# Gated attention with a routed layer behind it: the negated score maxima of a batch kept in one padded 128-column tile and turned by one product instead of four

## What is computed

```
Q = (layernorm(x) @ Wq.T + bq)            # 16 heads of 32
K, V = (ctx @ Wk.T + bk), (ctx @ Wv.T + bv)
attn = softmax(Q K^T / sqrt(32))
x = x + tanh(g_xattn) * ((mean_e(attn V @ We.T + be)) @ Wo.T + bo)
...
best = argmax(softmax(layernorm(x) @ w_gate)); place = running count of best
x = x + tanh(g_ffn) * gate * (layernorm(x) @ w_expert + b_expert)   # where place < 100
```

## Time and profile before

| | us |
|---|---|
| median of 3 runs | 409.02 |
| lowest and highest run | 408.29, 409.28 |
| span of the profiled execution | 406.7 |

### The profile page before, as it was taken

One profiled execution on the slowest core, in us unless ns is written; L12 is line 12 of the kernel. 1 busy time (PEld: TensorE's weight loads), 2 busy tenths in 40 slices (PEclk: granted clock), 3 DMA queues, 4 the chain that ended last, 5 costly groups with the idle time before them and its releaser, 6 DMA issues.

```text
span 406.7 us, 8772 instructions
## 1 busy us (share of the span) xinstructions
PE 400.1 (98%) x3126; PEld 190.6 (47%) x3126; DVE 336.5 (83%) x683; ACT 228.2 (56%) x320; POOL 167.0 (41%) x154
## 2 busy tenths in 40 slices
PE   8999999999999999999999999999999999999996
PEld 4556664444444444444444444444444444454444
DVE  6549566986897989988998999899897688779996
ACT  4435423678556764946585485748556473876110
POOL 2027999224171157309034530803261063460371
PEclk9999999999999999999999999999999999999999
DMA  7999991464058408814860683286059016241585
GB/s 266 319 388 396 366 382 39 104 126 148 2 129 194 158 12 168 233 68 98 145 236 2 149 228 106 65 175 240 0 131 238 9 33 172 79 135 27 96 167 185
DMA packets 65517, 63.19 MB, mean 155 GB/s; under 512 B 41765, under 2 KB 45233, under 8 KB 65475
## 3 DMA queue, kind: packets, MB, share of 16 engines
q1 hardware_dynamic: 60363, 56.19, 50.7%
q0 software_dynamic: 1632, 3.49, 3.2%
q10 hardware_dynamic: 3480, 2.96, 2.2%
HBM read 29.59 MB, written 12.98 MB: 105 GB/s over the span
## 4 chain that ended last, share of the span: by engine, by line
PE 93%; DVE 2%; ACT 1%; DMA 1%; issue 1%; SPq 0%; POOL 0%; ACTq 0%; DVEq 0%
PE ps L840 76%; PE ps L456 9%; PE ps L588 3%; PE ps L405 2%; DMA ctx_raw<-in_ctx_dram 1%; ACT probs L1237 1%; ACT mixT_hi L397 0%; SPq L729 0%; PE ps L1164 0%; DVE xb L1570 0%; DVE wqT_lo L1680 0%; DVE mixT_lo L398 0%; POOL known L1931 0%; PE ps L606 0%; PE ps L525 0%
## 5 line engine op out<-in xcount | busy, mean ns | idle before, releaser
L1237 ACT ACTIVATE probs<-ps 120x1024 f32<-120x1024 f32 x64 | 62.0, 1024 | 21.8 <-PE ps L840 21.7
L1604 DVE TENSOR_REDUCE neg_max<-ps 128x16 bf16<-128x1920 f32 x32 | 68.6, 2143 | 3.7 <-PE ps L840 3.7
L1990 POOL TENSOR_TENSOR attn_lo<-attn,attn_hi 128x512 f16<-128x512 f32 x28 | 31.8, 1158 | 91.3 <-ACT attn_hi L1237 91.3
L840 PE MATMUL ps<-xnT_hi,wqT_hi 128*128 128x512 f16 x128 | 48.6, 380 | 0.0
L840 PE MATMUL ps<-mixT_hi,attn_hi 128*128 128x512 f16 x128 | 48.6, 380 | 0.0
L840 PE MATMUL ps<-mixT_lo,attn_hi 128*128 128x512 f16 x128 | 48.5, 379 | 0.0
L840 PE MATMUL ps<-xnT_lo,wqT_hi 128*128 128x512 f16 x128 | 48.5, 379 | 0.0
L1998 POOL TENSOR_TENSOR xb<-xb,mix_bias 128x512 f32<-128x512 f32 x32 | 39.6, 1270 | 15.1 <-DVE cb_col L1547 15.1
L1237 ACT ACTIVATE q_hi<-ps,bias_cols 128x512 f16<-128x512 f32 x32 | 22.1, 689 | 31.5 <-PE ps L840 31.5
L840 PE MATMUL ps<-q_stack,k_stack 97*120 97x512 f16 x128 | 35.0, 390 | 1.2 <-DMA q_stack<-shift 0.7
L840 PE MATMUL ps<-probs,den_sel 120*32 120x256 f32 x512 | 34.1, 384 | 0.0
(11 more groups left out here) (277 smaller groups left out, 807.0 us busy)
## 6 DMA issues: line engine op xcount, KB each, us to landing
xb<-in_x_dram SPq DMA_DIRECT2D x8, 1024.0 KB, 7.0
q_stack<-q_hi SPq DMA_DIRECT2D x48, 128.0 KB, 2.4
out_dram<-xb SPq DMA_DIRECT2D x6, 1024.0 KB, 6.7
raw<-in_L_xattn_We_dram SPq DMA_DIRECT2D x5, 1024.0 KB, 11.2
q_stack<-q_lo SPq DMA_DIRECT2D x32, 128.0 KB, 2.6
xb<-in_L_xattn_We_dram SPq DMA_DIRECT2D x3, 1024.0 KB, 10.1
k_stack<-k_scratch SPq DMA_DIRECT2D x8, 360.0 KB, 4.4
k_scratch<-k_hi ACTq DMA_DIRECT2D x16, 120.0 KB, 7.2
```

Of the source, the lines that this page charges most:

```text
L840: return e.matmul(out_, a, b, start=start, stop=stop, **kw)
L1237: return e.activation(out_, in_, func, **kw)
L1604: e.tensor_reduce(neg_max[:, :, :, g], quad[:, :, 0:NT * SK].rearrange("p j (t s) -> p t j s", t=NT), AX.X, ALU.max, negate=True).then_inc ...
L1990: e.tensor_tensor(attn_lo[:, g, :], attn[:, g, :], attn_hi[:, g, :], ALU.subtract).then_inc(s_alo, 1)
```

## The change

- `neg_max` becomes one tile of 128 x 128 bf16. Columns 0 to 63 hold the maxima in the order (j, g, t), columns 64 to 127 are zeroed once at the start by GpSimd (one more MEMSET; the count SET that others wait for goes from 16 to 17).
- The reduction writes the same 16 numbers with other distances.
- max_turn is one product with all 128 columns as weights; its output is 128 x 128, of which 64 partitions matter.
- shift_row reads 64 x 128 instead of 16 x 512.
- The transfer into row 96 of `q_stack` reads 64 partitions of 256 bytes instead of 16 of 1024.

```diff
-        neg_max = sb("neg_max", [P, NT, HJ, NK], BF16)
-        shift = sb("shift", [H, S], F16)
+        neg_max = sb("neg_max", [P, P], BF16)
+        shift = sb("shift", [NT * H, P], F16)
...
-        SET, SETV, N_CONST = 16, 21, 1
+        SET, SETV, N_CONST = 17, 21, 1
...
-                    load(q_stack[3 * DK:STACK, :, :, :].rearrange("o j g s -> o (j g) s"),
+                    load(q_stack[3 * DK:STACK, :, :, :].rearrange("o j g (t s) -> o (j g t) s", s=P),
                          shift[:, :], s_rsh)
...
-                for t in range(NT):
-                    ins = mm(den_b[0:H, t * P:(t + 1) * P], neg_max[:, t, :, :].rearrange("p j g -> p (j g)"),
-                             ident_bf[:, :])
-                ins.then_inc(s_mt, 1)
+                mm(den_b[:, 0:P], neg_max[:, :], ident_bf[:, :]).then_inc(s_mt, 1)
...
-                act(shift[:, :], den_b[0:H, :], scale=1.0 / SHIFT_UNIT).then_inc(s_sh, 1)
+                act(shift[:, :], den_b[0:NT * H, 0:P], scale=1.0 / SHIFT_UNIT).then_inc(s_sh, 1)
...
-                e.tensor_reduce(neg_max[:, :, :, g], quad[:, :, 0:NT * SK].rearrange("p j (t s) -> p t j s", t=NT),
+                maxed = neg_max[:, 0:NT * H].rearrange("p (j g t) -> p t j g", j=HJ, g=NK)
+                e.tensor_reduce(maxed[:, :, :, g], quad[:, :, 0:NT * SK].rearrange("p j (t s) -> p t j s", t=NT),
                                 AX.X, ALU.max, negate=True).then_inc(s_mx, 1)
...
+            made_const(e.memset(neg_max[:, NT * H:P], 0.0))
```

## The result

The changed kernel takes **407.13 us** (median of 21 runs, 406.5 to 408.3); the kernel before, run beside it, takes 408.33 (407.8 to 409.38). The ratio is 0.9972 with a 95% interval from 0.9966 to 0.9978: 1.14 us less, certain in sign, and just under the 0.3% that a single comparison can tell. Forecast were 0.80 us less. The forecast time of 408.2 started from the 409.02 of three runs; from 408.33, the median of 21, the same 0.80 gives 407.5. The profiled execution after has a span of 405.5 us (before 406.7). The ratios of this document leave out three runs that fell far above the rest (415.65 and 588.33 of the kernel before, beside e1 to e4, and 1034.96 of e6).

A forecast was written before the change was run, and what follows sets the result against it. The prediction took TensorE (PE), busy for 98% of the span, as the bound, with DVE second in batches 2 to 6. It summed 0.30 + 5 x 0.12 - 0.10 = 0.80 us, so 409.02 - 0.8 = 408.2, range 406.9 to 409.2.

The forecast's parts named there:

- The turn, 0.30: PE at max_turn: one full-array product, without the 128*128 to 128*16 border, lets the next product start 0.30 us earlier.
- Batch 0, nothing kept: The product behind the turn waits for a part of sum_lo from DVE, not for the turn: 0 gained.
- Batch 1, 0.30: Scores of group 1 wait for exponentials that follow scores(1, 0), so everything behind moves along: 0.30 us kept.
- Batches 3 to 6, 0.12 each: At table_rows PE waits for DVE's place_hot, leaving 0.04; scores of group 1 return 0.08 to 0.10: 0.12 us each.
- Batch 2, 0.12: Same DVE limit at table_rows, with the shift's issue moving from 158.44 to about 157.91: 0.12 us kept.
- Batch 7, nothing kept and -0.10: scores(7, 0) waits for the shift's transfer, so the turn gives 0 and the slower transfer costs 0.10 us.
- Transfer +0.1: Shift into q_stack: 64 rows of 256 bytes take 0.1 us longer, hidden in batches 1 to 6, lost in batch 7.
- wide load 0: PE at the turn: loading 128 columns of weights instead of 16 costs nothing.
- The base, 409.02: Median time of the kernel before that the saving was subtracted from; the measured time was put 2.3 us above the span.
- A: Rival: DVE isn't second, six batches keep 0.30 to 0.36; 406.6 to 407.2 us; chance 0.20.
- B: Rival: nothing measurable, the turn shortens by three products alone, 0.16; saving 0.2 to 0.5, 408.5 to 408.9; chance 0.13.
- C: Rival: the shift's transfer becomes the bound, slower by up to 0.9; +1.3 us, 410.3; chance 0.09.

The follow-up runs named there:

- e1: The changed kernel run once more with the same instructions; 406.88 us, ratio 0.9970.
- e4: The changed kernel with DVE's three steps that lead to table_rows put before four it doesn't wait for; 407.00 us, ratio 0.9972.
- e6: The changed kernel with the shift's transfer issued by ACT behind its copy instead of by SP; 415.92 us, ratio 1.0165.
- e9: The changed kernel with DVE's steps toward table_rows earlier and ACT making three of twelve q_stack copies instead of two; 406.23 us, ratio 0.9957.
- e8: The kernel before, with shift padded so that its transfer has 64 pieces of 256 bytes; 408.15 us, ratio 1.0002.
- e2: Four products kept, each with 128 weight columns of which 16 matter, transfer and copy as before the change; 407.28 us, ratio 0.9979.
- e5: The changed kernel with six warm-up products of 512 columns on PE made 48 of 64 columns; 407.17 us, ratio 0.9972.
- e11: The changed kernel with its one product using 64 weight columns instead of 128; 407.33 us, ratio 0.9982.

## Why the prediction was right or wrong

- **The turn, 0.30: right.** 0.29, starting 0.05 behind the reduction. So are its parts: the border 0.2 where the turn waits for nothing and 0.14 beside the wait, the three products 0.16.
- **Batch 0, nothing kept: right.** The product behind the turn stands where `sum_lo` lets it (0 in every kernel).
- **Batch 1, 0.30: right.**
- **Batches 3 to 6, 0.12 each: right in mechanism** (e4 and e9 take the wait away and get the whole), 0.15 measured. The wait at table_rows takes 0.22 of the 0.29 and some 0.09 come back at the scores of group 1, against 0.26 and 0.08.
- **Batch 2, 0.12: wrong, -0.25 and -0.52.** The step that failed is that the issue moves from 158.44 "to about 157.91". It took SP as free whenever ACT is done. In before SP's four q_lo issues end at 154.60 + 3.33 = 157.93, 0.5 ahead of ACT: enough for ACT's old end, and nothing for the new one. With one of the four at 2.18 us instead of 1.43 the shift came 0.84 behind ACT. Of these 0.84 some 0.3 were covered, not the 0.53 that the prediction kept for the transfer, and the other 0.53 were lost.
- **Batch 7, nothing kept and -0.10: wrong, 0.36.** The step that failed is "PE's 0.30 becomes 0.30 more of waiting". It took the first wait of the batch for the one that sets its end, and the 4.0 us to landing of one execution for a fixed time: after landed 2.5 after its issue. In the same trace the values and scores behind it show no wait only because PE was late already. Kernels whose turn saves 0.29 keep 0.36 to 0.38, those that save 0.13 to 0.15 keep 0.21, those that save nothing 0.06 or 0.07, with and without a wait at scores(7, 0). The 0.06 that all have above before are the part of before's wait that the chain behind did not absorb; they are not the change's. The 0.30 come through because DVE's chain starts at a product behind the turn.
- **Transfer +0.1, ACT 0.27, wide load 0: right** (0.1 in the changed kernel and 0.16 in e8, without a wait; 0.27; e2 for the load). Nothing speaks against GpSimd's 0.
- **The base, 409.02: 0.7 too high.** Three runs gave it, 21 give 408.33. Nor do 2.3 us lie around the span: 407.26 - 405.5 = 1.8 in the kernel after. Of the 1.07 between 408.2 and 407.13, 0.69 are this and the rest is the saving.
- **Rivals.** A (kept whole) is what e9 shows once two limits are removed, not what the change did. B is out. C is out for this transfer, and its mechanism appeared in e6. Two of their prices were off: A's lower end is 409.02 - 2.2 - 0.43 = 406.4, not 406.6, and B's saving 0.16 + 5 x (0.04 to 0.12) - 0.10 = 0.26 to 0.66, not 0.2 to 0.5.

The sum: the two errors, -0.37 in batch 2 and +0.46 in batch 7, nearly cancel, and four small ones of 0.02 to 0.04 in batches 3 to 6 make up the rest of 1.01 - 0.80. The saving lies between 0.4 and 1.2 because the turn and DVE's place behind it were read correctly; that batch 2 and batch 7 made up for one another was luck. The time alone would have spoken for rival A, whose 406.6 to 407.2 hold 407.13: the base put it there, and the waits for DVE in the trace decide for the forecast.

## What to carry to other kernels

A first wait in a stretch is not what the stretch costs: go on to the next place where the engine waits, and ask whether the wait there would grow by as much as this one shrinks. When a step is made faster, follow each queue that it hands over to and read what that queue does at the new, earlier time, not whether it was idle at the old one. And two edits that are worth nothing alone (DVE's order, one copy to ACT) can be worth half as much as a change itself, or more, once that change is in: about 0.6 us, from 0.9972 to 0.9957 of 408.2 (the intervals just overlap), and 0.7 to 1.0 by the batches of the traces.

## What the hardware did that I had not expected

- An issue on SP that takes 0.59 us took 1.3 to 2.5 where a 16384-byte packet of the instruction queue ran at the same time; 42 more products at the start of PE's list moved both, together, to other batches (e5), with SP's own list unchanged. That the fetch causes the long issue is the likely reading, shown by their moving together; how, no run shows.
- Order between queues is part of a program: with a transpose issued 0.76 us ahead on SP, a 16 KB transfer from ACT's queue landed after 4.7 us instead of 2.1, its first packet 2.9 after the issue, and the kernel lost 6.7 us (e6), part of it in stretches of 3.4 us at half the clock behind waits of 2 us.
- A product of 128*64 pays the same border against 128*128 as one of 128*16: 0.09 us going in (batch 0) and about 0.1 coming out (e11).
